# Cross-attention on one core: the narrow products of two heads in one block, and the work around them reordered

## The reference, cut to what matters

```
x: (2, 2048, 512)   ctx: (2, 77, 384)   8 heads of 512
Q = x @ Wq ; K = ctx @ Wk ; V = ctx @ Wv            (per head)
score = Q K^T / sqrt(512), masked ; attn = softmax(score)
out = (attn V, heads side by side) @ Wo + x
result = layernorm(out) * gamma + beta
```

## Time and profile before

| | us |
|---|---|
| median of 3 runs | 348.5 (348.44 to 349.04) |
| profiled execution, its own time | 348.85 |
| its span in the trace | 347.0 |
| PE busy | 340.5 (98%) |
| DVE / ACT / POOL busy | 278.8 / 250.5 / 241.0 |

### The profile page before, as it was taken

How to read it: one execution, slowest core, us unless ns; L and a number is a source line. 1 busy time by engine, 2 the same in 40 slices (tenths; PEclk the granted TensorE clock), 3 DMA queues, 4 the chain that set the end, 5 groups by cost and what they waited for, 6 DMA issues and landing times.

```text
span 347.0 us, 7124 instructions
## 1 busy us (share of the span) xinstructions
PE 340.5 (98%) x2328; PEld 308.7 (89%) x2328; DVE 278.8 (80%) x515; ACT 250.5 (72%) x822; POOL 241.0 (69%) x252
## 2 busy tenths in 40 slices
PE   8999999999999999999999999999999999999994
PEld 5999999988888899889998899899989998998884
DVE  2159999488889677998798798887987978879896
ACT  2267774667888799797687886976978869769460
POOL 2044660599889989888868769688688696784243
PEclk9999999999999999999999999999999999999999
DMA  7998769788651080044144152241440522412012
GB/s 244 420 420 330 284 220 322 278 333 322 234 194 55 13 300 6 18 167 151 45 170 144 41 182 75 110 154 57 154 150 34 182 85 98 155 61 93 30 49 105
DMA packets 20101, 56.26 MB, mean 162 GB/s; under 512 B 1936, under 2 KB 3472, under 8 KB 18144
## 3 DMA queue, kind: packets, MB, share of 16 engines
q1 hardware_dynamic: 19200, 54.80, 43.3%
q10 hardware_dynamic: 864, 1.00, 0.8%
HBM read 46.98 MB, written 8.39 MB: 160 GB/s over the span
## 4 chain that ended last, share of the span: by engine, by line
PE 90%; ACT 5%; DMA 1%; DVE 1%; issue 1%; SPq 1%; DVEq 0%; POOL 0%
PE pair L801 30%; PE pair L724 23%; PE pair L604 13%; PE pair L597 11%; PE pair L696 6%; PE pair L783 4%; PE pair L714 2%; ACT prob L978 2%; DMA w_proj<-wk 1%; PE pair L818 1%; PE pair L786 1%; ACT prob L987 1%; SPq L546 1%; ACT xo_hi L1013 1%; ACT vw_hi L942 0%
## 5 line engine op out<-in xcount | busy, mean ns | idle before, releaser
L801 PE MATMUL pair<-vw_hi,pt_hi 128*128 128x512 f32 x155 | 62.2, 401 | 0.0
L801 PE MATMUL pair<-vw_hi,pt_lo 128*128 128x512 f32 x155 | 60.9, 393 | 0.0
L801 PE MATMUL pair<-vw_lo,pt_hi 128*128 128x512 f32 x155 | 60.6, 391 | 0.0
L1511 POOL TENSOR_TENSOR out_sb<-centred,beta_sb 128x512 f32<-128x512 f32 x30 | 38.8, 1292 | 30.3 <-ACT centred L1032 30.2
L987 ACT ACTIVATE prob<-c,neg_max 128x77 f32<-128x77 f32 x128 | 43.9, 346 | 0.0
L1556 POOL TENSOR_TENSOR xo_lo<-x_sum,xo_hi 128x512 fp32r<-128x512 f32 x32 | 41.4, 1299 | 0.0
L724 PE MATMUL pair<-a_hi,xo_hi 128*128 128x304 f32 x128 | 39.9, 312 | 0.6 <-ACT pair L965 0.6
L724 PE MATMUL pair<-a_lo,xo_hi 128*128 128x304 f32 x128 | 38.6, 302 | 0.0
L724 PE MATMUL pair<-a_hi,xo_lo 128*128 128x304 f32 x128 | 38.5, 301 | 0.0
L1025 ACT ACTIVATE pt_hi<-pair 128x640 fp32r<-128x640 f32 x32 | 22.5, 702 | 22.0 <-PE pair L786 22.0
L1575 POOL TENSOR_TENSOR w_proj_lo<-w_proj,w_proj_hi 128x768 fp32r<-128x768 f32 x10 | 18.4, 1863 | 28.3 <-ACT w_proj_hi L891 28.3
(11 more groups left out here) (138 smaller groups left out, 1054.4 us busy)
## 6 DMA issues: line engine op xcount, KB each, us to landing
w_out<-wo SPq DMA_DIRECT2D x8, 1024.0 KB, 5.0
xt_in<-x_tiles SPq DMA_DIRECT2D x16, 512.0 KB, 3.8
x_in<-x_rows SPq DMA_DIRECT2D x16, 512.0 KB, 4.8
out<-out_sb SPq DMA_DIRECT2D x31, 256.0 KB, 2.2
w_out<-wq_t SPq DMA_DIRECT2D x7, 1024.0 KB, 7.4
w_proj<-wv SPq DMA_DIRECT2D x8, 768.0 KB, 4.9
w_proj<-wk SPq DMA_DIRECT2D x6, 768.0 KB, 9.4
w_out<-wq_t SPq DMA_DIRECT2D x2, 512.0 KB, 7.9
```

What stands on the lines that cost most here:

```text
L801: mm = pe.matmul(ps_out[:, i % 2, 0:s.model], ps[:, j, :], v[:, j, b, :], start=(j == 0 and n == 0), stop=(j == s.key_t - 1 and n == len(p ...
L1511: pool.tensor_tensor(out_sb[i % OUT_RING][:, :], centred[i % 2][:, :], beta_sb[:, :], ALU.add)\
```

## The change

- **Narrow products in pairs.** `value_strips(u)` of an even u is followed at once by `value_strips(u + 1)`, ahead of the next projection and of `value_product(u + 1)`. Both heads write one PSUM bank, side by side. `take_strips` copies both heads (26 rows x 2 x 128 columns, 4 instructions) and runs 4 times instead of 8; `move_strips` issues 3 DMAs per pair of heads instead of 4. The last pair comes ahead of `value_product(15)`.
- **Score bank opened in the key half.** The matmul over ones, 312 columns between the last narrow products, becomes one over the 8 columns that were not written yet, in `out_product(7)`. `seed(0)` on ACT moves behind `take_strips(3)`.
- **Pair 0.** The order A11, S2, S1, A12, S3 becomes A11, S2, A12, S1, S3. ACT's `split_vw(7)` comes behind `copy_s1(0)`; `last_keys(0)` and half of `round_sums(1)` move into `exps_first(0)`. The low parts of S3, S4 and A22 of pair 0 go from POOL to DVE (`split_later_blocks`).
- **Order of the T sums, their roundings and splits** in the value half changes on ACT and DVE. POOL makes `v_rest` behind the first of the four pieces instead of behind the fourth.
- **Last key tile.** ACT's and POOL's `split_rest` come later: ACT's (0) behind `split_pt(0)`, POOL's (0) behind `block_sums(2)`. The products take 104 rows, and both `clear_pad` go.
- **Tile 1's split.** DVE's `split_pt(1)` comes ahead of `residual(0)`.

```diff
@@ PE
-                elif u < USES - 1:
-                    value_product(u)
-                    value_strips(u)
-                else:
-                    open_bank_a()
-                    value_strips(u)
-                    value_product(u)
+                else:
+                    value_product(u)
+                    if (u - H) % 2 == 0:
+                        value_strips(u)
+                        value_strips(u + 1)
...
-            first_products(0)
+            first_product(0)
+            product_s2(0)
             product_on_a(0)
+            product_s1(0)
             product_s3(0)
...
-                        mm = pe.matmul(ps_out[:, i % 2, 0:s.model], ps[:, j, :], v[:, j, b, :],
+                        mm = pe.matmul(ps_out[:, i % 2, 0:s.model], ps[0:rows, j, :], v[0:rows, j, b, :],
@@ ACT, behind round_w_out(u + 1), round_kv(u + 1) and split_vw(u - H)
                 if u == H:
                     round_t(T1, 0)
+                    take_strips(0)
                 elif u == H + 1:
+                    round_t(T3, 0)
                     round_t(T2, 0)
                 elif u == H + 2:
                     round_t(T4, 0)
+                    take_strips(1)
                 elif u == H + 3:
                     round_t(T1, 1)
                 elif u == H + 4:
+                    take_strips(2)
+                    round_t(T3, 1)
                     round_t(T2, 1)
                 elif u == H + 5:
                     round_t(T4, 1)
+                    round_blocks(0)
+                elif u == H + 6:
+                    round_sums(0)
+                    take_strips(3)
+                    seed(0)
+            round_blocks(1)
             copy_s1(0)
-            round_blocks(1)
-            split_rest(0)
-            last_keys(0)
-            round_sums(1)
+            split_vw(H - 1)
+            round_first_sums(1)
             exps_first(0)
             copy_s1(1)
             exps_second(0)
             split_pt(0)
-            split_rest(1)
+            split_rest(0)
@@ DVE, ahead of split_vw(u - H)
                 elif u == H + 4:
-                    right_sum(1, 5, 6)
                     split_t(T1, 1)
                 elif u == H + 5:
+                    split_t(T3, 1)
                     split_t(T2, 1)
                     right_sum(1, 6, 8)
+                elif u == H + 6:
+                    split_w_out(u + 1, range(0, 1))
+                elif u == H + 7:
+                    split_later_blocks()
                 split_vw(u - H)
...
                 elif u == H + 4:
-                    split_t(T3, 1)
-                    clear_pad(vw_lo)
+                    right_sum(1, 4, 6)
                 elif u == H + 5:
                     split_t(T4, 1)
                 elif u == H + 6:
-                    clear_pad(vw_hi)
+                    split_w_out(u + 1, range(1, 2))
...
             normalise(2)
+            split_pt(1)
             residual(0)
-            split_pt(1)
@@ POOL
+            for u in range(H, USES - 1):
+                split_values(u, 0)
+                add_rest_values(u)
+                for k in range(1, s.dim_t):
+                    split_values(u, k)
+            first_block_sum(0)
+            add_rest_values(USES - 1)
+            later_block_sums(0)
             split_block(0, A11, 2, 1)
             split_sums(0, S1, 3)
-            split_sums(0, S3, 4)
-            split_block(0, A22, 1, 2)
             ...
                     block_sums(p + 1)
+                    if p == 1:
+                        split_rest(0)
                     split_block(p + 1, A11, 2, 1)
...
-                if p < s.batches:
-                    split_rest(p)
+                if p == 1:
+                    split_rest(1)
```

More of the change, by code:

```diff
@@ L181, in build @@
         with ExitStack() as early:
-            strip_sb = [early.enter_context(nc.sbuf_tensor(f"strip_sb{n}", [P, s.model], F32)) for n in range(2)]
+            strip_sb = early.enter_context(nc.sbuf_tensor("strip_sb", [P, 2, s.model], F32))
         c12 = sb("c12", [P, s.half])
@@ L252, in build @@
         ld_x = [sem(f"ld_x{n}") for n in range(X_RING)]
-        ld_rest = [sem(f"ld_rest{n}") for n in range(2)]
+        ld_rest = sem("ld_rest")
         stored = [sem(f"stored{n}") for n in range(OUT_RING)]
@@ L539, in load_w_out, with move_strips @@
                     sp.dma_start(w_out_sb[u % W_RING][:, :, :, :], src).then_inc(ld_w_out[u % W_RING], DMA_INC)
[L541 to L547, removed]
+            def move_strips(pair):
+                h, rest_of = 2 * pair, s.rest
+                sp.wait_ge(act_strip, pair + 1)
+                sp.dma_start(rest_rows[place(h, 0) * rest_of:(place(h, 0) + 1) * rest_of, :, :],
+                             strip_sb[0:rest_of, :, :]).then_inc(ld_rest, DMA_INC)
+                for n in range(2):
+                    b = 1 - n
+                    to = place(h + n, b) * rest_of
+                    sp.dma_start(rest_rows[to:to + rest_of, b, :], strip_sb[rest_of:2 * rest_of, n, :])\
+                      .then_inc(ld_rest, DMA_INC)
             sp.dma_start(ctx_sb[:, :, :], ctx_t).then_inc(ld_ctx, DMA_INC)
@@ L563, in _ @@
                     load_xt(u - H - 2)
-            for h in range(H - W_RING, H):
-                move_strips(h)
+            for pair in range(2, H // 2):
+                move_strips(pair)
             sp.wait_ge(pe_outp, 2 * USES)
@@ L662, in out_product_full, with open_bank_a @@
                         mm.then_inc(pe_outp, 1)
+            def open_bank_a():
+                ends = slice(2 * s.kept_toks, HALF_HEADS * s.slot)
+                pe.matmul(bank_a[:, ends], ones[:, 0:P], ones[:, ends], start=False, stop=True, skip_group_check=True)
             def out_product(u):
                 wait_kv(u, 1)
+                if u == H - 1:
+                    open_bank_a()
                 for m in range(s.model_t):
@@ L728, in product, with first_product @@
                 mm.then_inc(pe_prod, 1)
[L730 to L738, removed]
+            def first_product(p):
                 b = batch_of(p)
@@ L1062, in _ @@
                     continue
-                if u == H + 1:
-                    round_t(T3, 0)
-                elif u == H + 4:
-                    round_t(T3, 1)
-                elif u == USES - 3:
-                    round_blocks(0)
-                elif u == USES - 1:
-                    seed(0)
-                    take_strips(u - H)
-                split_vw(u - H)
-                if u == USES - 2:
-                    round_sums(0)
                 if u < USES - 1:
-                    take_strips(u - H)
+                    split_vw(u - H)
                 if u == H:
                     round_t(T1, 0)
+                    take_strips(0)
                 elif u == H + 1:
+                    round_t(T3, 0)
                     round_t(T2, 0)
@@ L1390, in _ @@
             for u in range(USES):
-                if H <= u < USES - 1 and by_vector(u + 1):
-                    split_w_out(u + 1, range(0, 1))
                 if u + 1 < USES and not whole_out(u + 1):
                     split_kv(u + 1)
-                if H <= u < USES - 1 and by_vector(u + 1):
-                    split_w_out(u + 1, range(1, 2))
                 if u < H:
```

166 lines of the change are left out of this document (103 added, 63 removed).

## The result

| | before | after |
|---|---|---|
| median of 5 runs | 348.74 us | 354.54 us (354.15 to 354.77) |
| span of the profiled execution | 347.0 | 352.4 |
| PE busy | 340.5 | 341.4 |

The ratio is 1.0165, 95% interval 1.0151 to 1.018. The direction was as forecast, and so were the waits for DVE at value products 14 and 15 and for POOL at `out_rows(0)`. A third wait, 1.48 us for the seed, was not in the sum, and 354.54 lies above the range of 347.4 to 353.4.

The account below looks back on a forecast made before the run. PE, busy 98% of the span, was taken as the bound. Terms: -1.25 + 0.15 + 1.2 + 1.5 = +1.6 at A11, -0.1 in pair 0, +1.9 at out_rows(0), -0.3: +3.1 us, median 351.6, range 347.4 to 353.4.

Parts of the forecast that it names:

- Joined blocks: PE's narrow blocks in pairs, with the score bank opened in the key half: -1.25 us (-0.8 to -1.7) if nothing is late.
- v_rest of head 1: POOL makes it behind head 1's first weight piece, ready at 72.25 where PE wants it at 72.1: cost 0.15 us (0 to 0.9).
- Value product 14 waits for DVE: PE waits for DVE's split_vw(5), delayed by later ACT work and a new split_t: 1.2 us (0.7 to 1.7), start 111.5.
- Value product 15: PE waits for DVE's split_vw(6), done at 117.85: 1.5 us (1.0 to 1.9), start 117.9 instead of 116.28.
- The seed is ready just in time: ACT's seed ahead of A11 of pair 0, ready at 120.5: no wait, up to 0.5 us if POOL's operations stretch.
- Pair 0: New order from A11 to pair 1: the 0.57 us wait can go, S3 starts later; -0.1 us taken (-0.6 to +0.6).
- out_rows(0) waits for POOL: POOL's split_rest(0) stands behind the x load and four block sums: wait 1.9 us (0.8 to 2.8), start 135.75.
- Tile 1's split: DVE's split_pt(1) ahead of residual(0) removes the 0.27 us wait ahead of tile 2's transposes: -0.3 us (-0.27 to -0.4).
- 104 rows: Last key tile's products with fewer rows: 0 us, lower end 0 too, upper end a tiling mode switch at each tile.
- the rival of a tiling mode: 104 rows are a tiling mode of their own in every out_rows: +10.2 us over 32 tiles, 357 to 362; chance 0.03.

Follow-up runs that it names:

- e4_t_order: The changed kernel with batch 1's T3 sums, rounding and low part back where the kernel before had them on DVE and ACT: 352.64 us.
- e7_joined: The kernel before with only the joined narrow blocks, the bank opened in the key half and split_pt(1) early: 349.14 us against 348.75.
- e2_seed_first: The changed kernel with ACT's seed(0) ahead of sums and strips at u = 14, and the strips between the two roundings of sums: 353.04 us.
- e3_rest_early: The changed kernel with split_rest(0) ahead of exps_second(0) on ACT and ahead of the wait for pair 2's xt_in on POOL: 353.62 us.
- e6_split1: The kernel before with only DVE's split_pt(1) put ahead of residual(0): 348.33 us against 348.75, ratio 0.9993.
- e1_rows104: The kernel before with only the last key tile's products cut to 104 rows, the two clears kept: 349.11 us against 348.68, ratio 1.0014.

## Why the prediction was wrong in size, step by step

- **Joined blocks** (-1.25 us if nothing is late): right as far as it shows. 64 matmuls took 1.01 + 0.88 as forecast, the projection 3.15. In e4_t_order value product 14 is 0.5 earlier than in the kernel before, where the terms up to there gave 0.7. The terms of the last pair and of the opened bank were not measured alone. e7_joined shows that the gain is spent again even with the old orders.
- **v_rest of head 1**: forecast 0.15, measured 0.28. The first joined block takes 2.17 us (71.19 to 73.36) where the later ones take 1.89.
- **Value product 14 waits for DVE**: right in cause, e4_t_order shows it; too small in size. Forecast 1.2 us of wait, starting at 111.5. The projection ahead of it starts at 107.68 and takes 3.15, so PE was ready at 110.83 and waited 1.6 until 112.39 (the 1.32 in brackets is counted from the modelled end). The projection had itself come 0.3 late for want of DVE's `kv_t`, and e4_t_order gets 1.8 back. Of ACT's terms, the wait of 0.44 for T2's sum, which took 1.66, was left out, and the strips took 1.54 instead of 1.25:

```profile
101.46 1.54 ACT L971 ACTIVATE strip_sb<-pair 26x256 f32<-26x256 f32 x4 [0.70 <-PE pair L735]
...
104.13 0.68 ACT L1036 ACTIVATE t_hi<-pair 128x608 fp32r<-128x608 f32 x1 [0.44 <-DVE pair L1285]
```

- **Value product 15**: forecast 117.9, measured 118.34. `split_vw(6)` is done at 118.24, as in the forecast's account. A second wait ends level with it: the narrow block ahead of the product was idle 0.78 us for `v_rest` and is over 1.01 us after its start, at 118.22. Both hang on DVE's `split_kv(15)`, so neither alone is shown to be the one that counts:

```profile
117.21 1.08 PE L735 MATMUL pair<-w_out,v_rest 128*32 128x128 f32 x32 [0.78 <-POOL v_rest L1647]
```

- **"The seed is ready just in time ... up to 0.5 too late if POOL's operations stretch"**: this is the step that failed, a wait put at nothing. The forecast had `split_kv(15)` end at about 115.0, `v_rest` and three block sums at 118.3 and the seed ready at 120.5. `v_rest` could only start at 115.87, and the four took 4.4 us instead of 3.3, with 1.29 for `v_rest` and 1.74 for the fourth sum; they ended at 120.25. Roundings, strips and the seed queued behind them on ACT, the seed ran from 122.39 to 122.80, and A11 waited 1.48. Without this wait A11 would have come at 121.2 (118.34 and the 2.89 from product 15 to A11 of the earlier trace rows); it came at 122.90. e2_seed_first got 1.5 us back by order alone. With the wait gone that kernel takes 353.04, which lies inside the range. The trace of the kernel before already had `v_rest` at 1.37 and one of the sums at 1.74, where nothing of TensorE waited for them.
- **Pair 0**: forecast -0.1, measured 6.73 us from A11 to A11 instead of 6.62: +0.1, inside the bounds. One wait was traded for another, as the forecast described: the 0.57 ahead of pair 1 is gone, and S3 starts 4.1 us after A11 (forecast 3.8), waiting for DVE's u2. No experiment isolates it.

```profile
127.00 0.38 PE L745 MATMUL pair<-a_hi,xo_hi 128*128 128x304 f32 x1 [0.53 <-DVE u_w L1302]
```

- **out_rows(0) waits for POOL**: right in cause (e3_rest_early); forecast 1.9 us, measured 0.98. The x loads began at 124.87 instead of 122.4, since the strips stand behind the same late sums, but the tile landed 8.2 us later (133.03) and not 9.07. That part is luck: the same distance is between 8.1 and 9.3 us in the traces of this case in which POOL waits for it.
- **Tile 1's split**: forecast -0.3. Not confirmed: as e6_split1 shows, the 0.27 us that it was to remove belong to one execution of the kernel before.
- **104 rows**: forecast 0, with "the lower end is 0 too". Measured +0.48 over 28 tiles, in every kernel that has them. The 0.48 rules out the rival of a tiling mode, which would have cost 10 us. The Trainium skill, "TensorEngine Tiling (Array Packing)", section Tiling Modes, lists modes of 128, 64 and 32 rows; the 0.48 agrees with 104 rows being no mode of their own. My upper bound had nothing between 0 and that. Why fewer rows cost anything is not settled.

In sum, in us, each term as the growth of a distance in the timeline of PE:

| term | forecast | measured |
|---|---|---|
| start of value product 15 | +1.6 | +2.1 |
| the seed: from product 15 to A11 | 0 | +1.7 |
| pair 0 | -0.1 | +0.1 |
| `out_rows(0)` | +1.9 | +1.1 |
| to tile 2 | -0.3 | -0.2 |
| rows, tile 2 to tile 30 | 0 | +0.5 |

The seed is most of the difference; the smaller wait at `out_rows(0)` hides half of it. The two profiled executions differ by 5.3 us and the medians by 5.8. About 0.3 of that gap may be the wait for the late tile in the trace of the kernel before; the rest is not traced to a cause.

## What to carry to other kernels

A gain on the engine that is the bound has to be paid for by engines that feed it in a fixed order: write down, for each engine, the instruction that the bound waits for next and everything that stands ahead of it, and put what needs little (a seed, a low part that is ready) ahead of what waits. Where two engines share the work of one stage, take the stretched durations of the trace, not the shortest ones, for the operations that will now fall side by side. Price a change that "can't cost anything" by itself: 0.017 us a tile is 0.5 of the 5.8 us here. And before a short wait is booked as a gain, look for it in a second trace of the same order: the 0.27 us of this case was in one of four.

## What was not expected of the hardware

- Matmuls whose contraction has fewer than 128 rows were slightly slower to follow one another here: 0.712 instead of 0.694 us for three of 512 columns (e1_rows104), and 0.48 us over 28 tiles for 96, 104 and 120 rows alike.
- The same operation takes very different times when DVE and POOL both work: `v_rest` on POOL 0.38 to 1.37 us, a block sum of 256 columns 0.72 to 1.74, and 1024 columns of weights on DVE 1.21 to 2.30. In the rows shown, both of the long ones of POOL fall beside operations of DVE with no operand in PSUM, and the short ones all or almost all beside operations of DVE that read PSUM. No run separates the two cases.
